# Top-64 attention: the threshold search counts on TensorE instead of on ScalarE

## The reference, cut to what matters

```python
Q = (layernorm(x) @ Wq.T + bq).reshape(b, 16, 256, 16)     # b = 32
K = (ctx @ Wk.T + bk).reshape(b, 16, 256, 16)
V = (ctx @ Wv.T + bv).reshape(b, 16, 256, 16)
scores = einsum('bhqd,bhkd->bhqk', Q, K) / 4
topk_scores, topk_idx = top_k(scores, 64)                   # exactly 64 of 256 keys
probs = softmax(topk_scores)
attn = einsum('bhqk,bhqkd->bhqd', probs, V[topk_idx])
x = x + tanh(g_xattn) * (attn.reshape(b, s, e) @ Wo.T + bo)
x = x + tanh(g_ffn) * fp8_gemm(layernorm(x))                # 256 x 256
```

## Time and profile before

| | |
|---|---|
| median of 3 runs | 3272.49 us (3266.62 to 3277.44) |
| the profiled execution, its own time | 3268.81 us |
| its span in the profile | 3266.9 us |
| mean granted TensorE clock | 0.717 of full speed |

### The profile page before, as it was taken

The page is one execution under the profiler, slowest core; times in us unless marked ns, Lnnn a source line. Parts: engine busy times, 40 slices in busy tenths (PEclk is TensorE's granted clock), DMA queues, the critical chain, the costliest instruction groups (busy, mean ns, idle before and its releaser), DMA issues.

```text
span 3266.9 us, 51511 instructions
## 1 busy us (share of the span) xinstructions
PE 1780.4 (54%) x7952; PEld 950.5 (29%) x7952; DVE 2691.6 (82%) x11883; ACT 2730.3 (84%) x9638; POOL 966.1 (30%) x1174
## 2 busy tenths in 40 slices
PE   3245555555465555455556556564556556454555
PEld 2122233332233233232323333332233223232222
DVE  1678888888888888888888888888888888888884
ACT  1888888998788898797889998988798788997983
POOL 5122223233222233232233223333223233232112
PEclk8567677777677777776667777767676767777777
DMA  4223332223333223331233333223333133331211
GB/s 70 38 43 60 49 47 52 52 49 63 52 52 54 45 49 63 52 55 34 48 64 56 60 48 56 48 48 64 53 49 55 33 62 61 55 54 33 40 24 46
DMA packets 451902, 166.43 MB, mean 51 GB/s; under 512 B 245616, under 2 KB 451440, under 8 KB 451520
## 3 DMA queue, kind: packets, MB, share of 16 engines
q1 hardware_dynamic: 451136, 162.38, 28.4%
q0 software_dynamic: 384, 0.33, 0.1%
HBM read 102.57 MB, written 59.24 MB: 50 GB/s over the span
## 4 chain that ended last, share of the span: by engine, by line
DVE 36%; ACT 30%; issue 17%; PE 14%; DVEq 2%; POOL 1%; ACTq 0%; DMA 0%; SPq 0%; POOLq 0%; another core or an unknown queue 0%
ACT act_junk L880 22%; DVE masked L1151 5%; DVE score_sb L1047 4%; PE ps_o L731 4%; DVE following L1157 4%; DVE masked L1146 3%; ACT unfit L891 3%; ACT pT_sb L900 2%; PE ps_a L684 2%; DVE X L1083 2%; PE ps_b L675 2%; PE ps_e L712 1%; PE ps_a L686 1%; DVE chord L1115 1%; PE ps_e L716 1%
## 5 line engine op out<-in xcount | busy, mean ns | idle before, releaser
L880 ACT ACTIVATE act_junk<-score_sb,X 128x256 int8<-128x256 f32 x3840 | 1892.1, 503 | 211.3 <-DVE X L1121 183.2
L712 PE MATMUL ps_e<-qs,ks 99*128 99x256 bf16 x1024 | 348.2, 350 | 1321.7 <-ACT pT_sb L900 1321.7
L731 PE MATMUL ps_o<-pT_sb,v_aug 128*32 128x256 f32 x2048 | 766.4, 514 | 0.5 <-ACT pT_sb L900 0.5
L880 ACT ACTIVATION_READ_ACCUMULATOR act_junk<-score_sb,X 128x1 f32 x3840 | 755.0, 197 | 0.0
L891 ACT ACTIVATE unfit<-score_sb,thr 128x256 bf16<-128x256 f32 x1024 | 463.1, 504 | 218.0 <-DVEq L1241 214.6
L1047 DVE TENSOR_SCALAR_CACHE_REDUCE score_sb<-ps_s 128x256 f32<-128x256 f32 x1024 | 418.8, 415 | 142.1 <-PE ps_s L698 140.0
L712 PEld LDWEIGHTS ps_e<-qs,ks 99*128 99x128 bf16 x1024 | 121.9, 119 | 1403.6 <-ACT unfit L891 1199.5
L1146 DVE TENSOR_SCALAR_CACHE_REDUCE masked<-score_sb,X 128x256 f32<-128x256 f32 x1024 | 426.3, 472 | 19.1 <-DVE x_res L1294 8.4
L1157 DVE MAX8 following<-masked 128x8 f32<-128x256 f32 x1024 | 357.7, 409 | 1.7 <-issue 0.7
L540 POOL CAST split<-proj 128x512 bf16<-128x512 f32 x64 | 48.0, 750 | 1042.8 <-ACT proj L866 1027.2
L716 PE MATMUL ps_e<-dropb,unfit 128*128 128x128 bf16 x2048 | 355.9, 273 | 0.0
(11 more groups left out here) (158 smaller groups left out, 3332.8 us busy)
## 6 DMA issues: line engine op xcount, KB each, us to landing
rows<-q_scr SPq DMA_DIRECT2D x192, 128.0 KB, 5.1
rows<-k_scr SPq DMA_DIRECT2D x192, 128.0 KB, 5.0
o_scr<-o_sb SPq DMA_DIRECT2D x128, 128.0 KB, 2.7
q_scr<-split SPq DMA_DIRECT2D x32, 384.0 KB, 2.7
k_scr<-split SPq DMA_DIRECT2D x32, 384.0 KB, 2.7
x_in<-in_x SPq DMA_DIRECT2D x32, 256.0 KB, 3.1
ctx_sb<-in_ctx SPq DMA_DIRECT2D x32, 256.0 KB, 2.7
v_scr<-proj SPq DMA_DIRECT2D x32, 256.0 KB, 5.8
```

The costliest lines, as they stand in the source:

```text
L712: nc.tensor.matmul(ps_e[:, n % 2, kc * TOK:(kc + 1) * TOK], ks[u][:, h, 8 * kc:8 * kc + 8, :].rearrange("d j t -> d (j t)"), qs[u][:, h, : ...
L731: ins = nc.tensor.matmul(ps_o[32 * c:32 * c + 32, half * TOK:(half + 1) * TOK], v_aug[p][:, 2 * h + kc, :], pT_sb[:, n % 2, kc * TOK:(kc + ...
L880: ins = nc.scalar.activation(act_junk[:, t, :], score_sb[:, slot, t, :], ACT.Sign, scale=-1.0, bias=X[slot % 2][:, 0, t:t + 1], accum_out= ...
```

## The change

Steering counts are made on TensorE. `scores_by_key` multiplies the scores of a head transposed into one of three banks of `ps_t`, `less_thresholds` adds minus the thresholds in PSUM, `signs` on ScalarE takes one Sign of 128x512 a head, and `tally` multiplies the signs with a column of ones. The thresholds reach TensorE by a transpose, a negated copy on ScalarE into the bf16 tile `minus_x`, and a product with a column of the identity. The final count moves from VectorE to ScalarE (four tiles a round), and the masked product is one VectorE instruction a tile. `exponents` shares the three banks; the other small products share `ps_a`. The update steps of VectorE are no longer interleaved with score copies. `X` has four buffers.

```diff
-        X = [sb(f"X{k}", [P, 2, GT]) for k in range(2)]
+        X = [sb(f"X{k}", [P, 2, GT]) for k in range(RING)]
+        sign = sb("sign", [P, SIGNS, 2 * TOK], BF16)
+        minus_x = sb("minus_x", [GT, P], BF16)
...
+            def transpose_thresholds(i, slot, r):
+
+                pe.wait_ge(s_thr, GUIDES * i + r + 1)
+                pe.wait_ge(s_crd, GUIDES * i + r)
+                nc.tensor.transpose(ps_xt, X[slot][:, 0, :], ident[:]).then_inc(s_xt, 1)
+
+            def scores_by_key(u, g, n, bank):
+
+                h = head_of(g, n)
+                for kc in range(2):
+                    nc.tensor.matmul(ps_t[:, bank, kc * TOK:(kc + 1) * TOK],
+                                     ks[u][0:SPLITS, h, 8 * kc:8 * kc + 8, :].rearrange("d j t -> d (j t)"),
+                                     qs[u][0:SPLITS, h, :, :].rearrange("d j t -> d (j t)"), start=(kc == 0), stop=False,
+                                     skip_group_check=True)
+
+            def less_thresholds(i, r, n, bank):
+
+                if n == 0:
+                    pe.wait_ge(s_mx, GUIDES * i + r + 1)
+                both_chunks = minus_x[:].rearrange("t (o q) -> t o q", o=1).to_broadcast([GT, 2, P])
+                for jh in range(2):
+                    ins = nc.tensor.matmul(ps_t[:, bank, :].rearrange("p (c j q) -> p c j q", c=2, j=2)[:, :, jh, :],
+                                           identb[0:GT, 2 * n + jh:2 * n + jh + 1].to_broadcast([GT, P]), both_chunks,
+                                           start=False, stop=(jh == 1), skip_group_check=True)
+                ins.then_inc(s_R, 1)
+
+            def tally(i, par, r, n, buf):
+
+                pe.wait_ge(s_G, GUIDES * GH * i + GH * r + n + 1)
+                for jh in range(2):
+                    for kc in range(2):
+                        ins = nc.tensor.matmul(ps_cnt[par][:, 2 * n + jh:2 * n + jh + 1],
+                                               sign[:, buf, kc * TOK + jh * P:kc * TOK + jh * P + P], ones_b[:],
+                                               start=(kc == 0), stop=(kc == 1))
+                if n == GH - 1:
+                    ins.then_inc(s_cnt, 1)
...
+            def count_round(b, p, u, g, r, phase, first, second, last, middle):
...
+                scores_by_key(u, g, 0, bank[0])
+                scores_by_key(u, g, 1, bank[1])
+                less_thresholds(i, r, 0, bank[0])
+                less_thresholds(i, r, 1, bank[1])
+                if last:
+                    exponent_taken(*last)
+                for n in (2, 3):
+                    scores_by_key(u, g, n, bank[n])
+                    less_thresholds(i, r, n, bank[n])
+                    tally(i, slot % 2, r, n - 2, buf[n - 2])
+                if first:
+                    exponents(*first, bank[4], False)
+                if middle:
+                    middle()
+                for n in (4, 5):
+                    tally(i, slot % 2, r, n - 2, buf[n - 2])
+                    scores_by_key(u, g, n, bank[n + 1])
+                    less_thresholds(i, r, n, bank[n + 1])
+                if first:
+                    exponent_taken(*first)
+                for n in (6, 7):
+                    scores_by_key(u, g, n, bank[n + 1])
+                    less_thresholds(i, r, n, bank[n + 1])
+                    tally(i, slot % 2, r, n - 2, buf[n - 2])
+                if second:
+                    exponents(*second, bank[9], False)
+                for n in (6, 7):
+                    tally(i, slot % 2, r, n, buf[n])
...
-            def guide_counts(i, slot, r):
-
-                act.wait_ge(s_cnt, at(GUIDES * i + r))
-                act.wait_ge(s_thr, GUIDES * i + r + 1)
-                for t in range(ACT_TILES):
-                    ins = nc.scalar.activation(act_junk[:, t, :], score_sb[:, slot, t, :], ACT.Sign, scale=-1.0,
-                                               bias=X[slot % 2][:, 0, t:t + 1], accum_out=count[slot % 2][:, t:t + 1])
-                ins.then_inc(s_cnt, 1)
+            def negate_thresholds(i, r):
+
+                act.wait_ge(s_xt, GUIDES * i + r + 1)
+                nc.scalar.activation(minus_x[:], ps_xt, ACT.Copy, scale=-1.0).then_inc(s_mx, 1)
+
+            def signs(i, r, n, buf, bank):
+
+                act.wait_ge(s_R, GUIDES * GH * i + GH * r + n + 1)
+                nc.scalar.activation(sign[:, buf, :], ps_t[:, bank, :], ACT.Sign).then_inc(s_G, 1)
...
+                ins = nc.scalar.activation(act_junk[:, t % JUNK, :], score_sb[:, slot, t, :], ACT.Sign, scale=-1.0,
+                                           bias=X[slot][:, 0, t:t + 1], accum_out=final_count[:, t:t + 1])
...
-                nc.vector.tensor_tensor(x[:, 1, :], aim[:], count[slot % 2][:], ALU.subtract).then_inc(s_upd, 1)
+                nc.vector.tensor_scalar(x[:, 1, :], ps_cnt[slot % 2], TOK - 2 * AIM, None, ALU.add).then_inc(s_crd, 1)
...
-                    nc.vector.tensor_scalar(masked[:, k, :], score_sb[:, slot, t, :], X[slot % 2][:, 0, t:t + 1], None,
-                                            ALU.is_gt, ALU.add, accum_out=final_count[:, t:t + 1]).then_inc(s_fin, 1)
+                    nc.vector.scalar_tensor_tensor(masked[:, k, :], score_sb[:, slot, t, :], X[slot][:, 0, t:t + 1],
+                                                   score_sb[:, slot, t, :], ALU.is_le, ALU.mult).then_inc(s_fin, 1)
...
-                nc.vector.scalar_tensor_tensor(masked[:], masked[:], -BIG, scores,
-                                               ALU.mult, ALU.add).then_inc(s_fin, 1)
```

More of the change, by code:

```diff
@@ L442, in batch @@
                     spread_reciprocals(b - 2)
+                if has(1):
+                    store_values(b + 1)
                 if has(3):
@@ L654, in _, with transpose_tokens @@
             pe.wait_ge(s_wev, 4)
-            def front_transposes(b):
+            def transpose_tokens(b):
                 pe.wait_ge(s_xn[0], b + 1)
-                pe.wait_ge(s_ctx, 16 * b + 16)
[L659 to L666, removed]
@@ L696, in scores @@
                 pe.wait_ge(s_copied, at(H - 1))
+                if read is not None:
+                    pe.wait_ge(s_load, 2 * read + 1)
                 for jh in range(2):
@@ L781, in _ @@
                     scores(0, 0, g, n)
-            scores(1, 1, 0, 0)
-            def mix_stage(b, p, u, g, n, before):
-                h = earlier(b, p, u, g, n, MASK_LAG, before)
-                if h:
-                    exponents(*h)
-                h = earlier(b, p, u, g, n, MIX_LAG, before)
-                if h:
-                    mix(*h)
+            for n in range(2):
+                scores(1, 1, 0, n)
+            for r in range(GUIDES):
+                transpose_thresholds(0, 0, r)
+                count_round(0, 0, 0, 0, r, BANKS - 1, None, None, None, None)
@@ L822, in _ @@
             schedule(pe, batch)
-            sum_unsure(2 * NB - 1, NB - 2, NB - 3)
             LAST = (NB - 1) % OPS
-            for n in range(GH):
-                mix_stage(NB - 1, 1, LAST, 1, n, True)
+            for n in range(GH + MIX_LAG):
+                if n == 0:
+                    sum_unsure(2 * NB - 1, 16 * NB)
+                if n >= MIX_LAG:
+                    h = NB - 1, 1, LAST, 1, n - MIX_LAG
+                else:
+                    h = NB - 1, 1, LAST, 0, GH + n - MIX_LAG
+                exponents(*h, n % BANKS, True)
+                mix(*h)
@@ L1348, in batch @@
                         ending = final_thresholds(i, slot) if last else iter(())
-                        next(steps, None)
-                        for jh in range(2):
-                            next(ending, None)
-                            next(steps, None)
-                        for jh in range(2):
-                            next(ending, None)
-                            if has(1) and not last:
-                                copy_scores(i + 2, fresh, 2 * r + 1, jh)
-                            next(steps, None)
                         for _ in ending:
```

457 lines of the change are left out of this document (274 added, 183 removed).

## The result

The changed kernel takes 9305.79 us (median of four runs, 9303.22 to 9314.29) against 3270.86 us before (four runs): a ratio of 2.845, with a 95% interval from 2.840 to 2.850. The profiled execution of the changed kernel has a span of 9312.4 us. I had said 9800 us, with a range from 8500 to 10,600.

A forecast was written before the change was run, and what follows sets the result against it. No engine is full; a loop between engines bounds the kernel. 80 us to first thresholds, 62 and 50 for group 0, 9362 for groups 1 to 62 at 151, then 125, 96 and 40 give 9815, said as 9800; range 8500 to 10,600.

The forecast's parts named there:

- The cause: Steering counts use thresholds rounded to bf16, the final count exact ones: 814 rows in 562 of 1024 tiles are selected again.
- The settling: VectorE's repeated selection of unsure tiles, once a group: 8.80 us a tile plus 1.3 us between tiles, 91.4 us a group.
- The three rounds behind it: Rounds 1 to 3 of a group, after the tiles are selected again: 19.2, 20.7 and 11.7 us.
- a tally's four products: On TensorE, four weight loads with one-column products per head: 0.06 us each, 0.24 us a head.
- a score pair and a threshold pair: TensorE's score and threshold products for one head of the count: 0.44 us at the high clock, 0.86 at the low.
- the clock: TensorE's granted clock: low through round 1 and round 2's count, rising in round 2's eight-product piece, high in round 3.
- Rival A: Rounding costs no tile: seven stay selected again, a round takes 11.5 us, the whole 3184 to 3305 us; chance 0.07.
- Rival B: TensorE's clock is high soon after each settling: rounds 1 and 2 take 11.2 and 13 us, the whole 8,850; chance 0.15.
- Rival C: The tally's weight loads on TensorE are not hidden: 0.16 us a pair, 9 us more a group, 10,360 us; chance 0.15.
- its other form, the clock low throughout: TensorE's clock stays low through the whole group: 158 us a group, 10,250 us; within the same chance of 0.15.
- The signs: Expected in the profile: near 562 selections, some 4500 select instances at 0.43 and 0.41 us, masks waiting 90 us a group.
- Undisturbed rounds of 11 to 12 us: Expected in the profile: rounds that no repeated tile selection disturbs last 11 to 12 us each.

## Why the prediction was right, and what in it was wrong

**The cause** is as I had it, and now shown from both sides (9180 us with the rounding in the old kernel, 3765 without it in the new one). The 562 tiles that I got by following the steering on the reference's inputs are 563 instances in the trace, and all 64 groups settle. One wrong detail of the same arithmetic: with the rounding once more at the end I had 5 tiles, and the trace has 7.

**The settling** holds to 1%: transposition of round 1 at 99.5 us after that of round 0, measured 100.3 between the two negated copies; a tile with its gap 8.80 + 1.3 us, measured 10.09; the gap 747.0 / 563 = 1.33 us in the mean, the 64 longer first ones included. The masks wait 5604.2 / 64 = 88 us a group (I had 90).

**The three rounds behind it** are the term of the sum that was mis-sized: 19.2 + 20.7 + 11.7 = 51.6 us, measured 14.5 + 12.9 + 14.0 = 41.4. Over the 62 groups of the sum that is 632 us, more than the 494 us by which 9800 is too high; other terms were too small (the settling by 0.8 us a group, some 50 us in all) and took part of the error back, so the total is closer than its parts by luck. Three things are in it, as TensorE's timeline of after shows at the low clock:

```profile
4024.74 0.61 PE L743 MATMUL ps_t<-qs,ks 96*128 96x256 bf16 x2
4025.28 0.60 PE L754 MATMUL ps_t<-minus_x,identb 16*128 16x256 bf16 x2
4025.81 0.26 PE L764 MATMUL ps_c<-ones_b,sign 128*128 128x1 bf16 x4
4025.93 0.59 PE L743 MATMUL ps_t<-qs,ks 96*128 96x256 bf16 x2
```

First, a tally's four products take 4025.93 - 4025.81 = 0.12 us, at the full clock 0.11 as well (1927.31 - 1927.20 above). I had 0.24, twice that at the low clock, from a load with a 128-column product behind it; the lower bound, 0, was nearer. The upper bound was misread besides: I had 0.10 us for a load that nothing hides and named for it, but the mean of that line is 124 ns. Second, a score pair and a threshold pair take 4025.81 - 4024.74 = 1.07 us at the low clock and 0.63 at the full one, where I had 0.86 and 0.44: 0.2 us a head in the other direction, which no row of before could show, since there no weight tile of 16 rows stands beside one of 96. A head comes to 1.19 us at the low clock in place of my 1.34, and at the full one to 0.74 in place of 0.68. Third, the clock: I had it low for all of round 1 and up in the late piece of round 2. In the trace round 1 goes from 4023.2 to 4037.7, round 2 to 4049.7 and round 3 to 4066.7. The clock is 0.50 from 4022 to 4036, 1.00 from 4038 to 4044, and from 4056 on 0.50 again, with TensorE busy in nearly all of it. It came up earlier than I said, at the start of round 2, and did not stay up: over 57 groups its mean is 0.51 in round 1, 0.78 in round 2 and 0.69 in round 3, where I had the full clock. The fall near 4055 us comes with TensorE busy before and behind it:

```profile
4052.00:4054.00 2.00, 2.00 (x27) 1.12 (x26) 2.00 (x9) 2.00 (x6) 1.79 (x4) 1.00 0.37 43
4054.00:4056.00 2.00, 2.00 (x14) 0.60 (x12) 1.66 (x8) 2.00 (x7) 2.00 (x1) 0.59 0.16 16
4056.00:4058.00 2.00, 2.00 (x21) 1.69 (x21) 1.45 (x3) 1.52 (x4) 1.83 (x3) 0.50 0.33 33
```

**Rival A** did not come, but its price is the largest error of the text: 3184 to 3305 us, and 3765 when it was made true. In it I had every undisturbed round at 11.5 us with the full clock. There the clock is at 0.66 in the mean; it falls with TensorE busy, and the four intervals (means, as in the table above) are 15.5, 12.3, 14.1 and 14.2 us. I had weighed the clock only behind an idle stretch. So even with no more tiles coming back than before, this change was a loss of 15%, until the threshold product was given more rows.

The Trainium skill ("TensorE: Matmul & The Clock Gate", Why this matters for your kernels) tells to avoid long gaps in TensorE's work. Here the gaps were gone (2355 of 2400 us busy, 0.66) and the clock was lower than in before (1355 of 2400, 0.72): this advice was met and did not suffice.

**Rival B** did not come in the changed kernel; it came with 128 rows, and had the size right: 8850 us, measured 8827. Its rounds 1 to 3 were 11.2, 13 and 11.7 us and measured 12.2, 10.8 and 11.2, so their sum fits (35.9 and 34.1), not each of them. **Rival C** is refuted by the tally's 0.11 to 0.12 us; its other form, the clock low throughout, by the stretches above. **The signs** that I listed hold: 563 instances, 4504 at 428 and 408 ns, masks waiting about 90 us a group, a mean clock of 0.565. "Undisturbed rounds of 11 to 12 us" does not: 12.9 to 14.5.

## What to carry to other kernels

When a count moves to another engine, ask first at what precision its operand arrives there: a search steered at one threshold and settled at another pays for every row in between, and where the repair goes by tiles of 128 rows, 0.6% of the rows are half of the tiles. Count those rows on the inputs before timing anything. Then read TensorE's granted clock over the new steady state, not only behind its gaps, and look at the distance between neighbouring products: a few zero rows of weights may be worth more than a better order.

## What was not expected of the hardware

- Zero rows beside the real ones raised the granted clock: 0.66, 0.85, 0.86 and 0.93 with 16, 64, 96 and 128 rows in the threshold product, with less busy time each time.
- With 16 rows the clock fell to 0.50 while TensorE was busy without a break (near 4055 us in the changed kernel, with 2.00 of 2.00 us busy on either side) and stayed there so (14.00 of 14.00 us from 4056 to 4070). With 96 and 128 rows no fall came without idle time before it.
- A weight tile of 16 or 64 rows beside one of 96 leaves some 0.1 us a pair uncovered at either clock (medians of a score pair: 0.31 us at the full clock and 0.52 at the low one); one of 96 or 128 rows does not (0.22 and 0.38).
- A full weight load with a one-column product behind it goes by in 0.03 us in a row of them, at either clock (four of them in 0.12 us at the low clock and 0.11 at the full one).
